# FFN1 of a quantized adaLN FFN on one core: the last six token blocks multiplied in pairs by a seven-product scheme, on float16 integer steps, and late w2 chunks quantized earlier

## The reference, cut to what matters

```python
# x: (4, 1024, 512), cond: (4, 256), W: (1536, 512), w1: (2048, 512), w2: (512, 2048)
fused = concat([x, mean(x, axis=1), cond, cond], axis=-1)
rel = relu(fused @ W + b)                                  # (4, 1024, 512)
def quant_act(x):    s = max(max(x), EPS) / 255.0;  return clip(round(x / s), 0, 255) * s, s
def quant_weight(w): s = max(max(|w|, axis=1), EPS) / 127.0; return clip(round(w / s), -128, 127) * s, s
def quant_linear(x, w, b):
    xq, s_in = quant_act(x); wq, s_w = quant_weight(w)
    return einsum('btd,fd->btf', xq, wq) + round(b / (s_in * s_w)) * (s_in * s_w)
h = relu(quant_linear(rel, w1, b1))                        # FFN1, hidden width 2048
out = x + quant_linear(h, w2, b2)                          # FFN2
```

## Time and profile before

| what | value |
|---|---|
| median of the runs shown | 337.14 us (337.13 to 337.51, 3 runs) |
| the profiled execution | 338.56 us, span 336.7 us |
| PE busy | 328.4 us, 98% of the span |
| DVE busy | 272.5 us, 81% |
| ACT busy | 171.9 us, 51% |
| POOL busy | 31.4 us, 9% |
| PE clock granted | 1.00 in every stretch read |

### The profile page before, as it was taken

One profiled execution on the slowest core, in us unless ns is written; L12 is line 12 of the kernel. 1 busy time (PEld: TensorE's weight loads), 2 busy tenths in 40 slices (PEclk: granted clock), 3 DMA queues, 4 the chain that ended last, 5 costly groups with the idle time before them and its releaser, 6 DMA issues.

```text
span 336.7 us, 4687 instructions
## 1 busy us (share of the span) xinstructions
PE 328.4 (98%) x1554; PEld 187.2 (56%) x1554; DVE 272.5 (81%) x582; ACT 171.9 (51%) x270; POOL 31.4 (9%) x32
## 2 busy tenths in 40 slices
PE   6999999999999999999999999989999999999996
PEld 6888888888685444444444444434444444444444
DVE  1559998997827899999999999976568586595996
ACT  2423875568412999960200000059957859559800
POOL 1006334553200000000000000000000000000000
DMA  7959999999670186879997120049973599856416
GB/s 221 271 169 251 230 212 234 272 283 252 170 220 0 63 358 247 331 63 416 362 313 249 36 88 1 2 144 400 417 288 125 182 417 423 346 180 201 185 64 249
DMA packets 48481, 75.21 MB, mean 223 GB/s; under 512 B 18744, under 2 KB 31312, under 8 KB 43728
## 3 DMA queue, kind: packets, MB, share of 16 engines
q1 hardware_dynamic: 48272, 74.72, 71.1%
q10 hardware_dynamic: 192, 0.28, 0.5%
HBM read 45.63 MB, written 25.17 MB: 210 GB/s over the span
## 4 chain that ended last, share of the span: by engine, by line
PE 90%; DVE 7%; DMA 2%; issue 0%; SPq 0%; DVEq 0%
PE bank L512 29%; PE bank L469 26%; PE bank L369 26%; PE bank L533 4%; DVE hidden L794 4%; DMA x_in<-in_x_dram 2%; PE bank L484 2%; PE bank L364 1%; DVE wmax L674 1%; PE bank L479 1%; PE bank L436 1%; DVE steps L858 0%; PE bank L455 0%; PE bank L360 0%; DVE steps L752 0%
## 5 line engine op out<-in xcount | busy, mean ns | idle before, releaser
L469 PE MATMUL bank<-pool_r,w_t 128*128 (+1 forms) x480 | 104.1, 379 | 0.5 <-DVE hidden L794 0.4
L794 DVE TENSOR_SCALAR_CACHE_REDUCE hidden<-bank,qb,hmax 128x512 f32<-128x512 f32 x128 | 96.0, 812 | 2.6 <-PE bank L484 1.3
L608 ACT ACTIVATE steps<-hidden,s_quant 128x512 int16 (+1 forms) x124 | 76.8, 707 | 21.2 <-DVE w_t L825 11.2
L469 PEld LDWEIGHTS bank<-pool_r,w_t 128*128 128x128 bf16 x480 | 46.8, 98 | 57.6 <-DVE hidden L794 1.8
L512 PE MATMUL bank<-w_t 128*128 128x512 bf16 x256 | 56.2, 379 | 0.9 <-DVE w_t L860 0.9
L369 PE MATMUL bank<-x_hi,cw_hi 128*128 128x512 f32 x128 | 48.7, 396 | 0.0
L369 PE MATMUL bank<-x_lo,cw_hi 128*128 128x512 f32 x128 | 48.5, 390 | 0.0
L369 PE MATMUL bank<-x_hi,cw_lo 128*128 128x512 f32 x128 | 48.4, 389 | 0.0
L512 PEld LDWEIGHTS bank<-w_t 128*128 128x128 bf16 x256 | 24.8, 98 | 31.8 <-DVE w_t L860 1.5
L512 PE MATMUL bank<-w_t,pool_q 128*128 128x512 bf16 x192 | 41.9, 379 | 0.0
L349 POOL TENSOR_TENSOR x_lo<-hidden,x_hi 128x512 fp32r<-128x512 f32 x24 | 30.3, 1296 | 54.3 <-ACT x_hi L542 54.3
(11 more groups left out here) (102 smaller groups left out, 265.3 us busy)
## 6 DMA issues: line engine op xcount, KB each, us to landing
hidden_spill<-hidden SPq DMA_DIRECT2D x16, 1024.0 KB, 5.2
hidden<-hidden_spill SPq DMA_DIRECT2D x16, 1024.0 KB, 7.8
pool_q<-in_L_ffn_w_dram SPq DMA_DIRECT2D x8, 1024.0 KB, 7.1
pool_r<-in_x_dram SPq DMA_DIRECT2D x8, 1024.0 KB, 5.8
x_in<-in_x_dram SPq DMA_DIRECT2D x28, 256.0 KB, 5.5
out_dram<-pool_r SPq DMA_DIRECT2D x7, 1024.0 KB, 4.5
pool_r<-in_L_cond_W_dram SPq DMA_DIRECT2D x2, 1024.0 KB, 11.1
x_in<-in_x_dram SPq DMA_DIRECT2D x1, 1024.0 KB, 9.2
```

The costliest lines, as they stand in the source:

```text
L469: mm = pe.matmul(bank[ft % BANKS][:, :], w1_t[:, ft, k, :], act_q[:, bass.ds(n * (KD * TB) + k * TB, TB)], start=(k == 0), stop=(k == KD - 1))
L608: ins = act.activation(steps[:, q % 2, f, :], hidden[:, bass.ds(slot * HB + ft * TB, TB)], ACT.Copy, scale=s_quant[:, ft:ft + 1])
L794: dve.tensor_scalar(hidden[:, bass.ds(slot * HB + ft * TB, TB)], bank[ft % BANKS][:, :], qb1[:, ft:ft + 1], hmax[:, ft:ft + 1], ALU.add, A ...
```

## The change

Three things are done.

**The products.** With the activations of a pair of blocks cut in halves by token block (rows of X) and by contraction (columns), and w1 cut into `W11, W12, W21, W22` by slice half (ft 0 to 7, 8 to 15) and contraction half, four tiles come from seven quarter products of two 128x128x512 matmuls each, in place of eight. Blocks (2,3), (4,5) and (6,7) are the pairs (`PAIRS`); each has eight groups G of four tiles, and the last group of all is made plainly (`plain_tile`), so there are 23 groups (`GROUPS`). Four sums of w1 quarters (`WS`) and four sums of activation quarters for each pair (`XS`) are made on POOL (`sum_w`, `sum_x`). They are whole numbers in float16, as is all that was bfloat16. In a group, product 1 is copied with its bias from PSUM to `hidden` by ACT (`keep1`) and DVE adds product 2 (`take11`). Products 1 and 6 add up in one bank; ACT copies that (`keep_x`), DVE adds the bank of products 5 and 3 (`take12`). Product 7 goes onto the first bank, ACT has copied product 5 (`keep5`), DVE adds (`take22`). Product 4 goes onto the same bank and DVE takes it with its bias (`take21`). `add_tile` is a `tensor_tensor_reduce`, which reads one tile in SBUF and one in PSUM and keeps the maximum.

**The activations.** ACT rounds blocks 1 to 4 straight into `act_q` as int16, and DVE clips them there (`clip_act`, 128x2048). Blocks 6, 5 and 7 go as before, by uint8 and a cast.

**Late weights and the rest.** Chunks 6 and 7 are scaled by DVE, rounded by ACT and turned by SP in the relation's last block; chunk 7 uses `x_in`. The b2 row's division is done on 128x4 values, and the s2 and b2 rows go through DRAM together. The loads of the residual x in FFN1 are issued in the order 0, 2 (after group 15) and 1, 3 (at the end).

```diff
+        PAIRS = [(2, 2, 3), (4, 0, 1), (6, 2, 3)]
+        GROUPS = FG * len(PAIRS) - 1
+        R1, R2, R5 = (bank[0], bank[3], bank[6]), (bank[1], bank[4]), (bank[2], bank[5], bank[7])
...
+            def sum_w(f):
+                at = slice(2 * f, 2 * f + 2)
+                step(pool.tensor_tensor(WS[0][:, at], W21[:, at], W22[:, at], ALU.add))
+                step(pool.tensor_tensor(WS[1][:, at], WS[0][:, at], W11[:, at], ALU.subtract))
+                pool.tensor_tensor(WS[2][:, at], W11[:, at], W21[:, at], ALU.subtract).then_inc(ws_ready, 1)
+                pool.tensor_tensor(WS[3][:, at], W12[:, at], WS[1][:, at], ALU.subtract).then_inc(ws_ready, 1)
...
+            pool.wait_ge(act_q_ready, 1)
+            sum_w(0)
+            sum_w(1)
+            pool.wait_ge(act_q_ready, 3)
+            pool.wait_ge(first_act_ready, KD + 1)
+            sum_x(0)
+            sum_w(2)
+            sum_w(3)
+            pool.wait_ge(act_q_ready, 4)
+            pool.wait_ge(act_q_late, 2)
+            pool.wait_ge(h_done, 2 * FT)
+            sum_x(1)
+            pool.wait_ge(act_q_late, 3)
+            pool.wait_ge(p_done[4], FG)
+            sum_x(2)
...
+            for G in range(GROUPS):
+                if G >= 1:
+                    part6(G - 1)
+                part1(G)
+                if G >= 2:
+                    part4(G - 2)
+                part2(G)
+                part5(G)
+                if G >= 1:
+                    part7(G - 1)
+                    part3(G - 1)
...
+            def add_tile(slot, ft, y_bank, taken):
+                tile = hidden[:, slot * HB + ft * TB:slot * HB + (ft + 1) * TB]
+                dve.tensor_tensor_reduce(tile, tile, y_bank[:, :], 1.0, hmax[:, ft:ft + 1], ALU.add, ALU.max,
+                                         accum_out=hmax[:, ft:ft + 1]).then_inc(taken, 1)
...
+            for G in range(GROUPS):
...
+                if G >= 2:
+                    dve.wait_ge(c11_taken, G - 1)
+                    take12(G - 2)
+                    dve.wait_ge(c22_taken, G - 1)
+                    take21(G - 2)
...
+                take11(G)
+                if G >= 1:
...
+                    take22(G - 1)
...
+            take_h(0, {5: 2, 13: 3})
+            take_h(1, {5: 4})
...
-            for slot in range(SLOTS):
-                take_h(slot, slot, None)
-                if slot < NB - EARLY:
-                    scale_w(EARLY + slot)
...
+            scale_w(NB - 2)
             dve.wait_ge(bias_done, 1)
             dve.tensor_copy(bias_parts, XT[0][:, :]).then_inc(parts_ready, 1)
             take_relation(n, 0)
+            scale_w(NB - 1)
             take_relation(n, 1)
```

More of the change, by code:

```diff
@@ L10 @@
 F32R = mybir.dt.float32r
-BF16 = mybir.dt.bfloat16
+F16 = mybir.dt.float16
 I32 = mybir.dt.int32
@@ L284, in _ @@
[L284 to L292, removed]
+                    spill_quarter(n, q)
+            for par in range(2):
+                sp.wait_ge(spilled[par], 16 + 16 * FQ)
@@ L489, in _, with part @@
                 product1(0, ft)
-            for blocks in ((1, SLOTS), (SLOTS, NB)):
-                with pe.Fori(*blocks) as n:
-                    pe.wait_ge(act_q_ready, 1 + n + 1)
-                    for ft in range(FT):
-                        product1(n, ft)
-            pe.wait_ge(h_taken, FT * (NB - 1) + BANKS + 11)
+            pe.wait_ge(act_q_ready, 1)
+            for ft in range(FT):
+                product1(1, ft)
+            def part(i, G, w, v, to, start=False):
+                for k in range(HK):
+                    mm = pe.matmul(to[:, :], w[:, G % FG, k, :], v[:, k * TB:(k + 1) * TB],
+                                   start=(start and k == 0), stop=(k == HK - 1),
+                                   skip_group_check=not start)
+                mm.then_inc(p_done[i], 1)
@@ new lines, in part2, with part5 @@
+            def part2(G):
+                _, _, x21, _ = x_quarters(PAIRS[G // FG][0])
+                if G < 2:
+                    pe.wait_ge(h_taken, old_tile(3 * G + 1))
+                else:
+                    pe.wait_ge(c11_taken, G - 1)
+                part(2, G, W12, x21, R2[G % 2], start=True)
+            def part5(G):
+                pe.wait_ge(xs_ready, G // FG + 1)
+                if G < FG and G % 2 == 0:
+                    pe.wait_ge(ws_ready, G + 2)
+                if G < 3:
+                    pe.wait_ge(h_taken, old_tile((2, 5, 7)[G]))
+                else:
+                    pe.wait_ge(c12_taken, G - 2)
+                part(5, G, WS[0], XS[G // FG][0], R5[G % 3], start=True)
@@ new lines, in _, with plain_tile @@
+            for G in range(GROUPS):
[9 more added lines that the diff above has]
+                    part3(G - 1)
+            def plain_tile(n, ft, to):
+                for k in range(KD):
+                    mm = pe.matmul(to[:, :], w1_t[:, ft, k, :], act_q[:, (n * KD + k) * TB:(n * KD + k + 1) * TB],
+                                   start=(k == 0), stop=(k == KD - 1))
+                mm.then_inc(h_done, 1)
@@ new lines, in _ @@
+            last = GROUPS - 1
+            part6(last)
+            pe.wait_ge(c21_taken, last - 1)
+            plain_tile(NB - 2, FG - 1, R1[GROUPS % 3])
+            part4(last - 1)
+            part7(last)
+            pe.wait_ge(c11_taken, last)
+            plain_tile(NB - 1, FG - 1, R2[GROUPS % 2])
+            part3(last)
+            pe.wait_ge(c12_taken, last - 1)
+            plain_tile(NB - 2, FT - 1, R5[GROUPS % 3])
+            part4(last)
+            pe.wait_ge(c11_taken, last + 1)
@@ L598, in _ @@
-            for n in range(1, NB):
-                quantize_act(n)
-            act.wait_ge(first_act_ready, KD + 1)
-            for c in range(EARLY, NB):
-                quantize_w(c)
+                    act.activation(to[:, k * TB:(k + 1) * TB], raw[:, (n * KD + k) * TB:(n * KD + k + 1) * TB],
+                                   ACT.Identity, scale=s_in_inv[:, 0:1], bias=bias1_inv[:, k, n // 2:n // 2 + 1]
+                                   ).then_inc(act_steps_ready, 1)
+            for n in range(1, 5):
+                round_act(n, act_i[:, n * KD * TB:(n + 1) * KD * TB])
```

378 lines of the change are left out of this document (274 added, 104 removed).

## The result

The changed kernel takes 330.40 us (median of 4 runs, 329.18 to 330.61) beside 337.28 us before (337.13 to 337.51): ratio 0.9785, interval 0.977 to 0.980. The forecast was 330.8 us.

What follows compares the result with a forecast made beforehand. PE's matmuls were taken to bound FFN1, with DVE next. Terms -9.95 - 0.45 + 1.2 + 1.3 + 0.8 + 0.5 + 0.2 = -6.4 us took the median from 337.14 to 330.8 us, range 328.2 to 338.5.

Steps and rivals of the forecast that it cites:

- rival 1: FFN1 group loop: PE keeps the bound, new take at 0.70 us or less; 328.3 to 329.3 us, chance 0.25.
- 46 matmuls fewer: FFN1 pairs: 23 groups with 14 matmuls where 16 were, 0.216 us each; -9.95 us if PE stays the bound.
- the maxima and the b2 row's parts: FFN1: two 128x2048 maxima leave, -0.45 us; the b2 row's reciprocal and product leave DVE, 0.
- the round trip's pace: Group loop: take22, product 4, take21, take11 sum to 3.08 us, 0.05 above PE, over 23 turns; +1.2 us.
- the end of FFN1: After the loop's last part7 and part3: DVE's ten takes, 7.3 us, outlast PE's 5.6; +1.3 us over the old end.
- clips, POOL, fifth take: Clips between takes +0.8 us, POOL's first activation sum +0.5, and the fifth take waiting for late weights +0.2.
- Who sets the pace: Group loop: PE 3.03 us a turn, DVE 2.93 with the new take at 0.73, round trip 3.08, which sets it.
- The first two blocks: FFN1 blocks 0 and 1: clips of blocks 2, 3 and 4 between takes, slowed beside POOL, cost +0.8 us (0 to 2.5).
- a sign of a wrong mechanism: Stated test: the mechanism is wrong if PE idles on ACT's copies, or if FFN2 is no longer full.
- The relation's last block: Before FFN1: scaling of chunks 6 and 7 on DVE hidden, 1.5 us of room; fifth take's wait for weights +0.2.
- Rival 2: Group loop: the new take is slow and the kernel slower, 342.3 us at 0.95, 370 with two passes; chance 0.13.
- rival 4: Late weights: turns of chunks 6 and 7 or scale rows delay the fifth take 2 to 4 us; 333 to 335, chance 0.08.

Runs made afterwards that it cites:

- e1: Changed kernel with blocks 2 to 7 multiplied plainly, no sums on POOL or copies on ACT, residual x loads and spills block by block: 336.65 us, ratio 0.9982.
- e4: Changed kernel with the take of product 4 near the end of FFN1 moved behind the first plain tile's take: 328.87 us, ratio 0.9754.
- e7: Changed kernel with the two-input take's maximum started from constant 0, so no pointer scalar (second quantization scale altered): 328.99 us, ratio 0.9760.
- e2: Changed kernel with the two-input take's factor 1.0 read from an SBUF column, a second pointer scalar: 330.55 us, ratio 0.9791.
- e3: Changed kernel with block 4's clip moved from between block 1's takes to the start of group 3 of the loop: 328.33 us, ratio 0.9739.

## Why the prediction was right, and where it was not

The direction and the size came out, but 330.8 beside 330.4 is closer than the sum deserves. In like cases the forecast was -6.4 us and the change gave -7.9; chance in the first medians gave 1.1 of the 1.5 back. The mechanism of the loop was rival 1's: without the +1.2 the forecast's own sum is -7.6, and the 0.35 by which the loss at the maxima was taken too small makes it -7.95. Rival 1's own -7.9 came from other terms, a hidden front and an end of 0.9. By its terms:

| term | predicted | measured | by |
|---|---|---|---|
| 46 matmuls fewer | -9.95 | -9.93 | 46 x 0.216, pitch of e1 |
| the maxima and the b2 row's parts | -0.45 | -0.80 | e1 |
| the round trip's pace | +1.2 | 0 | turn 3.02 |
| the end of FFN1 | +1.3 | +1.26 | after, e4 |
| clips, POOL, fifth take (0.8 + 0.5 + 0.2) | +1.5 | +1.51 | two waits at the loop's beginning, 1.35 and 0.16 |
| sum | -6.4 | -7.96 | stage: -7.93 |

- *Who sets the pace.* The step that failed is "I take 0.73, since the form has a pointer scalar and an accumulator, as L794 has". L794 has two pointers, `qb1` and `hmax`; the new take has one. e7, after and e2 give 0.61, 0.67 and 0.73 for none, one and two. With 0.67 the round trip, put together from the pieces that e2 shows, is 0.74 + 0.07 + 0.60 + 0.13 + 0.73 + 0.67 = 2.94 us, which is less than the 3.02 of PE's 14 matmuls. The rest of that step held: e2 puts the take at 0.73 and gets the predicted turn, 0.05 us over PE's. So the loop went by **rival 1**. The estimate from the Trainium skill, Vector Engine (DVE) Microarchitecture Reference, section 5.2, was 0.61 us: exact for the form without a pointer, and 0.06 short of the form in this kernel.
- *The loss at the maxima* was -0.80, not -0.45. The prediction read it from busy time, and the starts show more (e1).
- *The end of FFN1.* The term's size is luck too. The ten takes cost 4 x 0.67 + 6 x 0.73 = 7.06 us, not 7.3. But DVE started them 0.04 ahead of PE, not 0.4, and it waited 0.71 for product 4 in between, which the prediction did not have (e4 takes 0.39 of it away). Against PE's 5.6 us that makes DVE 2.1 us the later. The prediction also named the take that followed the last matmul in the kernel before, but did not subtract it: by starts it held that end up by 0.93 us, and 2.1 less 0.9 is near the 1.26 measured.
- *The first two blocks.* The sum was right, the parts weren't. The three costs were each put at their own place, and PE lost nothing there. Of the three clips between takes one waited beside POOL, 0.58 us, where three waits of 1.2 were assumed. `sum_x(0)` was done at 133.22 and wanted at 135.32. The fifth take, at 115.45, had no idle time before it. PE was full to 135. Of the 1.51 us, 1.35 fell at a coupling that I had named in the step on the round trip but not at its first turn: product 4 wants DVE to be level with PE. e3 shows that the clip in block 1 is what put DVE late. The other 0.16 is a wait for ACT's copy, which the prediction had as hidden: in the first group only products 2 and 5 lie between product 1 and the product that needs the copy. PE idling on ACT's copies was also named as a sign of a wrong mechanism; it is seen at this one place. That the sum is equal is chance.
- *POOL.* Here each instruction was faster than I took. A 128x512 one in float16 took 1.16 us (I took 1.30, from float32), and one of 1024 columns 2.13, or 2.20 from start to start (I took 2.5 with its wait):

```profile
128.56 2.13 POOL L428 TENSOR_TENSOR steps<-pool_r 128x1024 f16<-128x1024 f16 x1
130.76 2.46 POOL L429 TENSOR_TENSOR steps<-pool_r,steps 128x1024 f16<-128x1024 f16 x1
133.18 1.15 POOL L417 TENSOR_TENSOR pool_q<-w_t 128x512 f16<-128x512 f16 x1
```

- *The relation's last block* was hidden, as predicted: both chunks' maxima (91.86 and 95.70) and still 1.13 us of rest before the last take, at 100.96. The room was predicted at 1.5.
- *Rival 2* (a slow take) is out: with one source in PSUM no halving shows, 0.61 us for 512 columns without a pointer. The rule of the Trainium skill, Vector Engine (DVE) Microarchitecture Reference, section 7, is for two SBUF sources and was not tested. Of *rival 4* nothing is seen: the fifth take did not wait.
- *The median.* I took the profiled execution's 1.4 us over the median for a constant. It was of the later of two cases, and three of the four runs of after are of that case as well.

## What to carry to other kernels

Count the pointer scalars when you take the pace of a new vector instruction from a neighbour, and read it from start to start. Where independent tiles give way to a loop in which PE waits for a take of its own group, the consumer's whole lag falls due at the first turn, so move side work behind that place. When two kernels' profiles differ before the first edited instruction, compare stage by stage.

## What was not expected of the hardware

- A 128x512 take costs 0.61 us from start to start without a pointer scalar, and 0.06 more for each one.
- One clip of 128x2048 took 1.27 us in place of 0.69, while POOL's instruction beside it took 2.46 in place of 2.13. Which of them holds the other was not separated.
- The first 11 us of most executions have one of two lengths, about 1.25 us apart, with some between. They go with the moment at which PE's matmuls reach their full pace, somewhere from before 5.5 us to 11 us, while the windows of the profile print a granted clock of 1.00 throughout.
